# Moving a stage's stack reads and a fill of ones in a four-block attention kernel, with a re-arranged table of steps

## The reference

```python
x = _L0_conv_ref(x, ...)  # xn = group_norm(x, 16 groups); 8 heads; softmax(q k^T * 16**-0.5) v; w_out + b_out; + x
x = _L1_conv_ref(x, ...)  # xn = group_norm(x, 32 groups); 8 heads; softmax(q k^T / 4) v; w_out + b_out; + xn
x = _L2_conv_ref(x, ...)  # layer_norm(x); 1 head; softmax(q k^T ...) v; Wp + bp; + x
x = _L3_conv_ref(x, ...)  # group_norm(x, 32 groups); 1 head; softmax(q k^T * 128**-0.5) v; wp + bp; + x
```

## Time and profile before

| | us |
|---|---|
| three runs, median | 2097.07 (2094.5 to 2097.71) |
| profiled execution, time | 2098.85 |
| profiled execution, span | 2097.1 |
| busy PE / DVE / ACT / POOL | 2034.3 / 1676.5 / 1490.4 / 413.9 |

### The profile page before, as it was taken

One profiled execution on the slowest core, in us unless ns is written; L12 is line 12 of the kernel. 1 busy time (PEld: TensorE's weight loads), 2 busy tenths in 40 slices (PEclk: granted clock), 3 DMA queues, 4 the chain that ended last, 5 costly groups with the idle time before them and its releaser, 6 DMA issues.

```text
span 2097.1 us, 40849 instructions
## 1 busy us (share of the span) xinstructions
PE 2034.3 (97%) x15800; PEld 1147.0 (55%) x15800; DVE 1676.5 (80%) x3104; ACT 1490.4 (71%) x2722; POOL 413.9 (20%) x544
## 2 busy tenths in 40 slices
PE   4799999999999999999999999999999999999999
PEld 3344444444744468444873448644585446846988
DVE  6799999999799978898789876898878977773433
ACT  1387788888588854988569874698747986597555
POOL 5002021220122311113120221203111031031231
PEclk7799999999999999999999999999999999999999
DMA  5401351412041314031230502305031040000000
GB/s 148 92 12 40 74 102 31 83 55 49 29 84 39 65 31 81 12 77 27 56 67 2 102 2 57 66 2 102 2 87 27 2 99 4 7 7 2 11 1 21
DMA packets 48592, 97.42 MB, mean 46 GB/s; under 512 B 7824, under 2 KB 10640, under 8 KB 48272
## 3 DMA queue, kind: packets, MB, share of 16 engines
q1 hardware_dynamic: 48400, 94.81, 21.1%
HBM read 55.98 MB, written 37.75 MB: 45 GB/s over the span
## 4 chain that ended last, share of the span: by engine, by line
PE 82%; DVE 10%; DMA 3%; ACT 2%; issue 2%; SPq 1%; POOL 1%; POOLq 0%; DVEq 0%; ACTq 0%
PE outs L1473 19%; PE banks L1435 14%; PE banks L1448 12%; PE outs L1513 11%; PE banks L1491 9%; DVE part_max L1227 8%; PE banks L1354 7%; PE banks L1360 5%; PE banks L1363 4%; ACT probs L1117 2%; DMA q_stack<-shift_parts 2%; SPq L904 0%; DMA q_scratch<-parts 0%; DVE o_turn L1239 0%; DVE stats L1166 0%
## 5 line engine op out<-in xcount | busy, mean ns | idle before, releaser
L1227 DVE TENSOR_REDUCE part_max<-banks 128x1 f32<-128x512 f32 x2048 | 1271.1, 680 | 166.6 <-PE banks L1435 161.4
L1117 ACT ACTIVATE probs<-banks 128x512 f32<-128x512 f32 x2048 | 1060.4, 611 | 200.0 <-PE banks L1448 172.8
L1473 PE MATMUL outs<-probs,v_heads 128*32 128x512 f32 (+1 forms) x5112 | 563.6, 522 | 0.8
L1435 PE MATMUL banks<-k_stack,q_stack 62*128 62x512 f32 x2048 | 550.9, 443 | 4.0 <-DVE part_max L1227 1.3
L1448 PE MATMUL banks<-q_stack,k_stack 64*128 64x512 f32 x2048 | 519.1, 444 | 21.4 <-DMA q_stack<-shift_parts 20.5
L1435 PEld LDWEIGHTS banks<-k_stack,q_stack 62*128 62x128 f32 x2048 | 257.4, 187 | 282.3 <-DVE part_max L1227 114.9
L1448 PEld LDWEIGHTS banks<-q_stack,k_stack 64*128 64x128 f32 x2048 | 244.0, 186 | 236.5 <-ACT probs L1117 77.2
L1124 ACT ACTIVATE probs<-banks,neg_max 128x1024 f32<-128x1024 f32 x128 | 142.7, 1115 | 220.9 <-DVE neg_max L1259 184.7
L1513 PEld LDWEIGHTS outs<-v_full,probs 128*128 128x128 f32 x2048 | 257.4, 191 | 47.0 <-issue 37.2
L1513 PE MATMUL outs<-v_full,probs 128*128 128x128 f32 x2048 | 276.8, 279 | 0.0
L1259 DVE TENSOR_REDUCE neg_max<-banks 128x1 f32<-128x1024 f32 x128 | 156.3, 1223 | 134.0 <-PE banks L1491 133.0
(11 more groups left out here) (107 smaller groups left out, 1160.3 us busy)
## 6 DMA issues: line engine op xcount, KB each, us to landing
k_scratch<-parts SPq DMA_DIRECT2D x64, 256.0 KB
q_scratch<-parts SPq DMA_DIRECT2D x64, 256.0 KB
k_stack<-k_scratch SPq DMA_DIRECT2D x64, 256.0 KB, 6.9
q_stack<-q_scratch SPq DMA_DIRECT2D x64, 256.0 KB, 8.2
k_stack<-k_scratch SPq DMA_DIRECT2D x64, 128.0 KB, 8.2
q_stack<-q_scratch SPq DMA_DIRECT2D x64, 128.0 KB, 9.7
q_stack<-shift_parts SPq DMA_DIRECT2D x256, 4.0 KB
...
```

Of the source, the lines that this page charges most:

```text
L1117: nc.scalar.activation(probs[:, plan.prob[u], 2 * n + half, :], banks[:, plan.banks["pair", t][k], :], ACT.Exp, scale=HEAD_SCALE).then_inc ...
L1227: nc.vector.tensor_reduce(part_max[:, r % 2, column:column + 1], bank_of(("tile", r, n)), AX_X, ALU.max, negate=True).then_inc(tile_max, 1)
L1435: nc.tensor.matmul(bank_of(("tile", r, n)), qs[rows, i, a, heads, P * t:P * (t + 1)], ks[rows, i, keys, heads, :], start=True, stop=True). ...
L1473: last = nc.tensor.matmul(outs[2 * HD * n:2 * HD * (n + 1), columns], v_heads[:, i, key, at:at + 2 * HD], probs[:, plan.prob[u], n, column ...
```

## The change

The reads k0, q0 and k1 of the second stage leave the prologue's list and are put into beats 3 and 5 of the first stage. The fill of ones of the second half follows POOL's split of q0 of image 1, not that of q1 of image 0. The strings FIRST_STEPS and STEPS are written anew: the three C of the reads go from the prologue's end, and three C stand before the first pair; by the queue's order these are now the projection q1 of image 1, its write, and the read k0; the reads q0 and k1 take the places that q1's projection and write had among the pairs, and the read q1 stays where it was. Some twenty other places of STEPS, all over the kernel, have their letters in another order; each class's own order stays, but 3 values steps more are whole (V) and not in halves (U).

```diff
-    FIRST_STEPS = "C" * 29 + "T" * 8 + "C" * 1 + "T" * 4 + "C" * 2 + "T" * 4 + "C" * 2 + "T" * 4 + "C" * 2 + "T" * 4 + "C" * 1 + "T" * 4 + "C" * 3 + "T" * 8 + "H" * 1 + "T" * 4
+    FIRST_STEPS = "C" * 29 + "T" * 8 + "C" * 1 + "T" * 4 + "C" * 2 + "T" * 4 + "C" * 2 + "T" * 4 + "C" * 2 + "T" * 4 + "C" * 1 + "T" * 12 + "H" * 1 + "T" * 4
...
-        "TPTPTTTPTUTPTU TTPTUTPTU TTPTUTPTU TTPTCUTPTU TTPTCUTPTU HTPTUTPTU TTPTPUTTU TPTPCUTTU CTPTTPTV TPTTPV "
+        "TCCCPTPTTTPTUTPTU TTPTUTPTU TTPTUTPTU TTPTCUTPTU TTPTCUTPTU HTPTUTPTU TTPTPUTTU TPTPCUTTU CTPTTPTV TPTTPV "
...
-        "TCPPTV PTTTTCPTTV PPCV HPTTUPTPTU CTTTPTV CTTTPPV PCCTTTTUCCCTPTTU PTTPV TTPTTCUPTTTPCCCU TTPTPV TPTTCTCCHV "
+        "TCPPTV PTTTTCPTTV PPCV HPTTUPTPTU CTPTTTCV TTTPPV PCCTTTTCCUTTTPTTU CCV PPTTTTPUPTTTPCCCU TTPTTCV TTPCCV "
...
-        "UCCPTPTU V PCTPTTV PTTPV PTTTPV CHTPTTPV CPTTTPV TTPCTTPUCCTPPTU UU TTPTPV PCTTPTCV TPTPTV CTPTPTV TPTTPV "
+        "UCCPTPTU V PCTPTTV PTTPV PTTTPV CHTPTTPV CPTTTPV TTPCTPTTTTTTTV UU CCPPPPV CPTTPCV PTTPTV CTPTPTV TPTTPV "
...
-        "TCTPTCTV PTTPCUU CPTTPUU PTTPV TPPTTUCU HPTTTPV CTPTTTTCCCPV PTTPV PTTPTV TPTTPV CPTTPCV TPTTPV CPTTPTV "
+        "TCTPTCTV PTTPCUU CPTTPUU PTTPV TPPTTUCU HPTTTPV CTPTTTTCCCPTPTPPTTPV TV TTV V TTPTPCCTPPV PTTPV CPTTPTV "
...
-        "CPPTTTV TPCTPTUTTTPTTU V CPCHPPPPPV V PCCCV V PCCV CCCTTTPPTTPPV PPTTCCV PTTPUU TTPTPV TTPPCV TTPTPV PTTPV "
+        "CPPTTTV TPTCTUU CPTTPTV PPTTV PPV HPPCCCCV PPCCV V CPTPTTCCTPTPV TTPPCV CPTTPUU TTPTPV TTPPCV TTPTPV PTTPV "
...
@@ -280,7 +280,8 @@
             if i == 1:
                 self.chain(h(0, 1), 0, i, ["q1"])
                 put(h(0, 2), ("write", 1, SPLIT.index("q1")))
-                put(h(0, 5), ("read", 1, "q1"))
+                put(h(0, 3), ("read", 1, "k0"), ("read", 1, "q0"))
+                put(h(0, 5), ("read", 1, "k1"), ("read", 1, "q1"))
                 self.available[1] = h(0, 1)
@@ -402,7 +403,6 @@
             at += 4
             if n in SPLIT:
                 order.append(("write", 1, SPLIT.index(n)))
-        order += [("read", 1, n) for n in ("k0", "q0", "k1")]
         return order + tiles[at:]
@@ -1043,7 +1043,7 @@
                     elif name in SPLIT:
                         split(name, layer, i)
-                        if (name, layer, i) == ("q1", 0, 0):
+                        if (name, layer, i) == ("q0", 0, 1):
                             pool.wait_ge(*split_done(name, layer, i))
                             fill_ones(1)
                             pool.wait_ge(ones_ready[1], 2)
```

More of the change, by code:

```diff
@@ L153 @@
+        "HTPTTTCPTTUPTTPU TTPUTTPCCCTCTU TTPPV CPTTPV TTPTTUU TPTPUTTPU TPTTTV PPTTV HPTPTTTV TPTPTTTTTTUU UU "
+        "TPTPTCCTTPUPCU TPTPV TTPTPV CCTTPTPV TTTTPUU TTPCHCPTPTTTUPPTTU TTTCTV PTTUTTPPU CCTTPTV TPTTTCCPTTV TTTPPV "
         "CCCTTTPTUCCCTTPTTCU TPTTV CHTTPTTCPTTUPTTCU TPPTCCV TPPV CCCPTPTTV CTPTPTUTTPU CTPTPTTTUTPTTU V TTTPTCV "
         "TPHPTTTTTPTV UPTPTTU TTPPTV CTPPTTUU PTPTTV TTPTPV TTPPTUTPTU TTPTHUPTTTTPTTU V PTTTPTV TPPTTV CTPPTTV "
[L155 removed]
@@ L156 @@
-        "TTPTTCTTPCCCUCTPTTPU TTTPTUU HTTTTCCCPCCPTPV V CTTPTPCUTTTCPPU CTTPPTV PCTPCV PTTTTV CTTPV TPTTTCPTTV "
+        "PTTTPTV PPCTTTV TPTTUPTPTU TPTCUHTPTTTU PTTV PTTPV TTTPPV CCTPPTTTTV PTTPUTTTTCCCCCU TPTTPV "
+        "TTPTTCPTTCCCTPPTTTTV HPTTV TTTTCCCCCPPPTCV V CTTPTPCUTTTCPPU CTTPPTV PCTPCV PTTTTV CTTPV TPTTTCPTTV "
         "TPTTTCHCTPTTTV PTTV TTPTTCPTTV CTPPTCUPTTTTCPTTU PTTCV TPTTPV PTPTTV HTTPTV TPTPTTTV PTPTTTCTPTTV PPCTV "
-        "CPPTTTUU PTTTPPTUTTTPU UCCPTPTTU UTTPCCHU TTTPCTV PTPTTTV TPTPV TTPTTV PTPTCCPTTTTV PTTV PTTTTCCCCCTPTPV "
+        "CPPTTTUU PTTTPPTUTTTPU UCCPTPTTU UTTPCCHU TPTTTV PPCTTUTTU TTPPV TTTPTV TPPTCCPTTTTV PTTV PTTTTCCCCCTPTPV "
@@ L159 @@
         "TPTTTUCCTPTTTTCCCPTTU PTTHCTPCTCUTPPTTU UU TPTCCV TPTTPV CCPTTPCUU TPPTTV TPTTPUCTPTCPTU TPTTV HTPTTTV "
[L160 to L163, removed]
+        "PTPPTTTTPTV V TTTTTPPUU CPTTPV TPTTPTTV TPTPTUTPTTU PTTPV TTPTHV TPTPTTTV TTPTPV TPTTPUU CPTTPTV PTTPCV "
@@ L164 @@
+        "TPTTPV TPTTPUTTPU TTPCPTTV PTTPV PTTTTV HSV CTTSR CSCR GGGTTTTTTTGGGR SGTTTSGYR SGR SGCGGGTTTTTTTGGCGCR "
+        "CYSGTTTTTGGGCTTCR PTTGGGGCR YCHCTPTTTGGGGCGGTTPTTGGCYTPTCPTTUCCPPU V PPCCCTTTV TPCPTV PTTCPV TPPTV "
+        "TPTTTTCTTV PTPTUTTPCU CCPTTTTV PTTV PTTHCTTPTTCUPTTTPCTPTTU PTTTTV PTTV PTTPCCV TPTTPV TPTPV CPPTTTV "
         "TPTTHCTTPTV TPTTCPV PPTTV PTTUTPTU CTTPPTV CTPTPTTTV TPPTV CCPTTTPV TTPUTPTU HTTPPTV CPTTPTCPTTTV TTPPV "
         "TPTTTUU PTTPV PTTPV CPTTTTCUPTTU TPTPUCCTPTTTCU CHTPTV PCTTPUCTTPTTU CTCTPTV PPTTCCCCCTTPCTTV TPTCV PTTPV "
-        "PPCCTTTV TTPPTV CTPTTPTTV PTTUPTTPU CTTHCCTTPUU CTPPTTV TPPTV TPTTPV CPTTPCV TPTTPUTTPTPU CTTPTV TPTTCPV "
@@ L167 @@
-        "TPTTTHPV UPTPTU CPTTTTCV TPTV PPTTCCCTTTPTV CPTTCTTPPCV PTTTV TTPPCTTPV TPTPV PPTTV V HTTPTSV CSTTTR CTTTR "
-        "SGTTTTGCGSGR SGSGGGR YTTGCGR SGGTTTTGGGCTTTTGCCYR SGGSGGCR CGGGTTTTTTTGCYCCR SGSGGGCR GGGTTTGCYR "
+        "PPCCTTTV TPPTTV CTPTTPV TPTTTUPTTPU CTTHCCTTPUCTPU PTPTTTV PTV V PTTPCPTTPCV TPTTPUTTPTPU CTTPTV TPTTCPV "
+        "TPTTTHPV UPTPTU CPTTTTCV TPTV PPTTCCCTTTPTV CPTTCTTPPCV PTTTV TTPPCTTPV TPTPV PPTTV V HPTTTSV CSTTTR TTTTCR "
+        "SGTTTCGGGR SSGSGR GGYSR GGGTTGCGTTTTTTGCGTTGCYCR SGSGGGCR GCGGTTTTTTTGCYCCR SGSGGGCR GGGTTTGCYR "
@@ L174 @@
-        "CHPPTTCV CPTTPV TTTTPCCTTPTTV CCPTTPUTTPU CCTPTPV PTTTTV TPTCPTTV TPTPV TPPTV PTTTV TTPSUU CHSR SCTR "
-        "GGTTTTTGSGSGR CGTTGGYSGR CGTTTTGR GSGCGTTTTGGCYR SGGGCGTTTTTTCGCGGR SGCR CYSCGTTTTGGGSCGR TTGGGCR "
+        "HPTTUPTTTTU CCTTPPCV PTTV TPTPCUTTPTTCU TPTTPV PTTPV CTPTPV PTTTPV PTTPTV TPTTPCV PTTPTV HTPPTUTTPU TTTCTPV "
+        "PCTTPUU PPCTTTV TPTTPV CPTTPTV CTPTTPV TCPTTPV TPTPTV PTTPTV HTPPTTV CPTTTPV PTTUTPTPU TPTTUU CPTTPTUU "
+        "PPTTCV TTPTPV TTPPV TPTTTV CPPTTCV HPTTPTCCTPTTTV CPCCPTTV CPTTPCTTTTCCV CTPPTTTTV PPTTCV CPCCTTPUU "
@@ L176 @@
+        "TPTTPCCV CPTTPV CPTTTPV HPTTPTTV CTPTTPV PTV TPTTTTPTCCCPTTPPUU TTV TPPUU CPTTPCV TTTPPV CTPTTPV TPTTPV "
+        "TPTPTV CHPPTTCV CPTTPV TTTTPCCTTPTTV CCPTTPUTTPU CCTPTPV PTTTTV TPTCPTTV TPTPV TPPTV PTTTV TTPSUU CHSR SCTR "
+        "GGTTTTTGSGSGR CGTTGGYSGR CGTTTTGR GSGCGTTTTGGCYR SGGGCGTTTTTTCGCGGR SGCR CYSGCTTTTGGGCR SGTTGGGCR "
         "YTTTTTGSGHCSGGCR CGTTGGGCCR YCSCGTTTTTGGGGGR R GGYTTTTSGSGTTGGR PCTTGGGGYCTTR TTPGGGGGGPTTGGYTTTPTCV PTTPTV "
```

20 lines of the change are left out of this document (7 added, 13 removed).

## The result

The changed kernel takes 2081.16 us, the median of four runs (2080.4 to 2084.53). The kernel before, run beside it, took 2095.78 (2089.77 to 2097.71). The ratio is 0.9937 [0.9921, 0.9953]. The forecast was 2081.8 with a range of 2074 to 2089.

A forecast was written before the change was run, and what follows sets the result against it. PE was taken to bound the body, with nearly all winnable idle time in the prologue. 10.8 (first pair) + 0.5 (q1's projection) + 4.0 (table) = 15.3 us; 2097.07 - 15.3 = 2081.8 us, range 2074 to 2089.

The forecast's parts named there:

- The fill, 3.8 us at the first tile: Prologue: moving POOL's fill frees DVE, columns ready 5.5 us earlier; first score tile at 39.8, not 43.62, waiting for q_stack's read.
- The maxima beside the fill: At about 52 to 59 us, DVE's maxima beside POOL's moved memsets were taken as not slowed, still 0.60 us each.
- The rival that holds them up: Between 52 and 59 us the moved fill stops DVE's maxima for 7.1 us; gain only 8.2 us, 2088.9; chance 0.06.
- The shift: Before the first pair: shift_parts ready at 63.0, sent ahead of the reads, first pair at 68.2, 10.8 us earlier than 79.02.
- q1's projection: Projection q1 runs on PE in the wait before the first pair instead of at 93.01: 0.5 us counted.
- The second shift finds an empty queue: q1's write and the reads, 2.75 MB, occupy the queue from 67 to 84; the second shift, issued at 88.9, follows them.
- The table, 4.0 us counted: Re-ordered STEPS in the body: 5.2 us from waits and whole values steps, counted as 4.0; ends 2 lost, 10 won.
- Counted at 216, 1207, 1459 and 1720: PE's later waits, three for shift rows and one for row maxima, shortened by 1.9, 0.4, 1.6 and 0.8 us.
- PE's clock came back: Rival: after the body's waits PE's granted clock recovers too, three places giving 5 us; 21.5 us in all, 2075.6; chance 0.12.
- the rival of the bursts: Body: tiles in a row starve ACT of pairs; 0.57 us at each of twenty places cancels 11.3 us; chance 0.05.
- one of my signs of being wrong: At the re-ordered places, DVE or ACT idle grows by more than PE's waits shrink.

The follow-up runs named there:

- the fill alone: Kernel before with only the second half's fill of ones moved behind POOL's split of q0 of image 1: 2095.12 us, ratio 1.0001.
- both edits: Kernel before with the fill of ones and the second stage's reads moved, all other rows of STEPS old: 2086.72 us, ratio 0.9956.
- the reads alone: Kernel before with the second stage's reads moved (FIRST_STEPS, first row of STEPS, planner's list), the fill of ones at its old place: 2087.62 us, ratio 0.9971.
- the mixed table: Changed kernel with five stretches of STEPS set back to their old letters: 2078.76 us, ratio 0.992; on another chip 2078.88 us, ratio 0.9905.
- the table alone: Kernel before with the other rows of STEPS new; FIRST_STEPS, first row of STEPS, reads and fill old: 2093.83 us, ratio 0.9997.
- the fill in pieces: Kernel before with the second fill of ones at its old place, cut from two memsets into eight: 2099.99 us in one run.

## Why the prediction was right, point by point

- **The fill, 3.8 us at the first tile: 2.7.** The columns were ready 5.2 us earlier, at 30.2 (forecast 5.5), and the first tile then waited for q_stack's last read, as forecast: the trace tells the wait as "issue", but this read, issued at 32.9, landed 7.9 us later, at 40.8. In this execution the loads ahead of it landed later: PE's first long wait, for the averages, was 5.2 us and not 4.5, and the last read was issued 0.9 us later than in the earlier trace rows. So 40.92 and not 39.8. In the run of the fill alone it was 40.71; there the read went out on time, at 31.9, and took 8.7 us to land.
- **The maxima beside the fill: not slowed**, 0.60 us. The rival that holds them up is out.
- **The shift: 68.2 forecast, 67.64 measured.** The parts came at 63.7 and not at 63.0, for the reason above, but PE waited only 1.2 us beyond the last issue's end where I counted 2.5. That 2.5 was measured behind a loaded queue. The two misses partly cancel: 11.4 against 10.8. PE's wait there was 1.85 us and not some 4.
- **q1's projection: 0.5 counted, 0.4 to 0.5 measured.** From the first pair to the second shift 0.7 and 1.5 us were won, with both edits and in the kernel after, but most of that goes with the clock (below).
- **The second shift finds an empty queue: right, with no room to spare.** The write and the reads ran from about 69 to 87, where I had 67 to 84 (DMA share 0.07 over 69 to 70, 0.99 over 84 to 86, 0.41 over 86 to 88), and the shift went out at 86.81, as they ended, without a wait of PE behind it.
- **The table, 4.0 us counted: 4.4 in the traces, but not from where I said.** Counted at 216, 1207, 1459 and 1720: 1.9, 0.4, 1.6 and 0.8. Won, by the lead around each: 1.5, 3.4, -0.8 and 4.5. The other places cost 4.2. So the sum was right by luck, because errors offset. No wait for shift rows was left in the body, where I had some 4 us.

The lead grows from 11.4 us at the first pair to 12.85 at the second shift, where I counted 0.5 for q1's projection. Busy time by stretch behind the first pair, first of the kernel before, then of both edits of the prologue, then of the kernel after:

```profile
79.00:84.00 5.00, 4.98 (x23) 2.75 (x23) 3.08 (x5) 3.05 (x6) 0.00 (x0) 0.50 0.00 0
84.00:89.00 5.00, 5.00 (x37) 1.68 (x33) 3.72 (x6) 2.68 (x6) 0.00 (x0) 0.62 0.00 0
```

```profile
67.50:72.50 5.00, 5.00 (x23) 2.59 (x23) 3.21 (x6) 3.15 (x7) 0.82 (x1) 0.50 0.41 93
72.50:77.50 5.00, 5.00 (x37) 1.89 (x37) 3.94 (x7) 2.94 (x6) 0.00 (x0) 0.67 1.00 185
```

```profile
67.60:72.60 5.00, 4.96 (x23) 2.75 (x23) 3.08 (x5) 3.05 (x6) 1.02 (x1) 0.50 0.39 91
72.60:77.60 5.00, 5.00 (x46) 2.06 (x44) 4.56 (x8) 3.36 (x7) 0.00 (x0) 0.91 1.00 187
```

PE starts at the half clock in each, 0.50, and gets the full one back at different times: the second five microseconds have 0.62, 0.67 and 0.91. Over all twelve traces the growth goes with this clock: 2.0 to 2.2 us where the second five microseconds have 1.00 (the fill alone, the reads alone and the first run of the mixed table), 1.0 to 1.6 at 0.81 to 0.93 (the three runs of the kernel after), 0.2 to 0.9 at 0.66 to 0.72. The fill alone has its 2.0 us with no edit between the first pair and the second shift. What is q1's is read at equal clocks: 0.9 in the second run of the mixed table and 0.5 in the table alone, which leaves q1 in its old place (both 0.50 and 0.72); 0.7 with both edits and 0.2 with the fill in pieces (0.66 and 0.67). That makes 0.4 to 0.5 us, as counted. The rest of the 1.5 goes with the earlier clock.

Two steps explain most of the table's places. First, PE's clock came back at three of the four, which I had put into a rival. Busy time by stretch of the kernel before, at the last of the four places:

```profile
1720.00:1730.00 10.00, 10.00 (x59) 3.02 (x62) 0.28 (x1) 7.34 (x16) 3.60 (x7) 0.83 1.03 178
```

and of the kernel after, at the second, the third and the last:

```profile
1195.00:1200.00 5.00, 4.02 (x36) 1.60 (x34) 3.47 (x8) 4.94 (x11) 0.60 (x1) 1.00 0.01 3
...
1441.00:1446.00 5.00, 4.53 (x22) 1.17 (x22) 2.97 (x5) 2.56 (x6) 1.88 (x2) 0.66 0.03 9
...
1708.00:1718.00 10.00, 9.95 (x77) 3.35 (x76) 1.96 (x5) 9.08 (x20) 4.43 (x6) 1.00 0.48 106
```

Where PE had stood waiting the granted clock had been 0.74, 0.66 and 0.83; at the second and the last place it is now 1.00. At the third it is 0.66 still, at another point of the same round: the wait is gone, but the lead falls by 0.8. From shift to shift around its place the kernel before loses 1.7 us to the clock at each of the four (a mean of 0.96 over 47.6 us, 0.94 over 29.8, 0.94 over 27.3 and 0.98 over 88.3); of these the kernel after loses as much at the third alone. At 1720 a wait of 0.84 us thus cost 1.7 us more in clock (10 us at 0.83); the other 2 of the 4.5 us won there are not accounted for. At 1207 I had left three of 3.63 us of wait standing; the new order left none for shift rows in this execution, and 0.9 and 1.0 in two others.

Second, the rival of the bursts is real, only smaller than its price. At round 19 the new order sets two whole values steps and five tiles in a row before the next pair (V V TTTTT). ACT's waits there in the kernel after, 469 to 499 us:

```profile
ACT probs L1117 <- PE banks L1448: 8.3, 7, 4.1
```

and in the kernel before at the same work, 484 to 510:

```profile
ACT probs L1117 <- PE banks L1448: 4.1, 7, 1.0
```

The four microseconds more of ACT's idle time go with the 3.7 of the step down. But 3.7 is the size in this one execution. PE's busy time by stretch there, in the kernel after:

```profile
473.00:475.00 2.00, 2.00 (x13) 0.60 (x16) 0.85 (x2) 0.53 (x2) 0.00 (x0) 0.50 0.08 11
```

and in the run of the same kernel beside the mixed table:

```profile
473.00:475.00 2.00, 2.00 (x20) 0.65 (x14) 0.52 (x1) 0.23 (x1) 0.00 (x0) 1.00 0.00 0
```

The clock fell in the first (0.93 from shift to shift, 1.7 us of its 24.7) and not in the second. The second and two more executions of this order, at 1.00 throughout, lose 2.1 us at round 19 (I had expected the step again within 0.5), and ACT waits 6.6 to 6.7 us there. So the order costs 2.1 us at this place, and ACT's idle time did grow where PE had no wait to lose, one of my signs of being wrong; over the whole body it does not outweigh the waits.

The rival needed twenty such places at 0.57 us to cancel the prologue. The four traces of the new order share four fixed steps down: 2.1 at 19, 2.0 at 27, 1.3 at 35 and 0.7 to 0.9 at 51. That the re-arranged letters cost the time is shown for 19 and 51, where the old letters win it back in both pairs of traces; at 51 most of it is the clock, 0.94 from shift to shift with the new letters in four traces and 1.00 with the old ones in two. For 35 it is open (2.1 won, 0.4 lost). For 27 it is not shown: no letters were set back, and the old order mostly loses there too. That a burst starves ACT is seen at 19 alone.

**What stays open.** By medians the prologue alone has the ratio 0.9956 and the rest alone 0.9997, intervals of 0.003 to 0.004 wide; the kernel after has 0.9937, 0.9932 and 0.9923 in three sessions. These add up within their intervals, but how much of the 14.6 us between the medians is the table's can't be told. The two traces have 12.8 and 4.4, for one execution each, and the waits that the table removes depend on when the transfers land in that execution. From the shift of round 5 to that of round 63 the lead changes by -4.9 to +9.2 us in five more executions with the old order, and by +4.3 to +6.2 in the four with the new one: steadier, and some 5 us better in the mean than the six of the old order, whose own spread is 14.
